# Attention b's output turned round by VectorE in blocks of 32 × 32 instead of by TensorE, in a kernel of four chained layers

## The chip, the cores and the metric

The kernel runs on one core of one Trainium2 chip. The metric is device time in microseconds (us), the median of several runs. Lower is better.

## The reference, cut to what matters

`x` has 4 batches × 256 tokens × 512 channels, in fp32. Four layers follow one another, each on the layernorm of `x` and added to `x`:

```
x = x + attn_a(layernorm(x))      # one head of 128
x = x + ffn(layernorm(x))         # int4 weights, dequantised
x = x + attn_b(layernorm(x))      # 32 heads of 16, rotary, causal
x = x + ffn(layernorm(x))         # the same weights again
# inside attn_b, for every batch:
q, k, v = x @ wq, x @ wk, x @ wv            # 512 -> 32 heads x 16
scores  = rotary(q) @ rotary(k).T / 4       # causal mask
out     = softmax(scores) @ v               # b, 256 tokens, 512
return out @ wo
# inside ffn: weight = (nibbles - zero) * scale, 512 x 512
```

## The kernel before, in words

Tokens lie on the 128 partitions, two tiles of 128 (t = 0, 1) to a batch. To multiply with a weight, the normalised activations `XN` are turned round by TensorE (step T), copied to `XT_hi` by ScalarE (TH, rounded to a short fp32 form) and the rest taken to `XT_lo` by VectorE (TL). Products then are two or three passes of TensorE over high and low parts (L816 to L818, L908 and L909).

Everything that is done is one step of a long hand-written list, `PLAN`, some 1,000 entries. Each engine walks through the list and issues its own steps in that order; waits between engines are semaphores, so an engine that waits holds up everything behind it in the list. `D` steps are loads, `OS` stores of the result, both on SyncE's queue. A function deals PSUM banks out in turn in the order of the list; in attention b's stretch three banks are kept for scores (S), three for the transposed scores (ST), and the other two serve all else.

Attention b works in 16 units u of 8 heads (four units for a batch), and each unit in two groups g of four heads:

- PJ projects queries and keys, RO, RP, P1, R1, P2, P3 apply the rotary table and split into three bf16 parts, SS and SL carry the parts through DRAM into `QK`. VP and VV make the values, 16 columns of values and 16 of ones for each head.
- S (L950, L952) makes scores and MX (L781) takes row maxima; MT, M1, M2, SM bring the maxima into `QK` as extra rows.
- ST (L973, L975) makes transposed scores less their maxima, EX (L667) exponentiates on ScalarE, MK (L547) masks on GpSimd, PV (L987) multiplies with the values. PV's result has 32 partitions for each of four heads (16 channels, and 16 rows that all hold the sum of the exponentials) and 256 tokens on the free axis.
- OU (ScalarE, two copies a unit, `OU`), NT (TensorE, L999, four transposes of 128 × 128 a unit) and NR (VectorE, L795 and L800: one reciprocal and two products) bring this to tokens on partitions and divide, into `O`.
- With all four units of a batch in `O`, DT (TensorE, L850, four transposes for each t), DH (ScalarE) and DL (VectorE, L720) turn it back to channels on partitions, high and low; WO (12 matmuls for each t, L816 to L818, 512 columns) multiplies with wo, OD (L757) adds to `X`.

Then layernorm LN (L714, L715), RS on GpSimd (four small steps with a power), NO on ScalarE (`XN`), T, TH, TL, the product F (L908, L909), and FS, FD (L744, L751, L753) on VectorE finish the batch, with BA (L515) on GpSimd. WT turns the int4 weights round once at the start (16 transposes, L835) after DQ unpacked them, and KP runs idle matmuls (L826) at the very start. The last steps of the list are those of batch 3.

## Time and profile before

| | |
|---|---|
| median of 3 runs | 287.44 us (287.19 to 287.57) |
| the profiled execution: own time, span | 289.1 us, 287.3 us |
| TensorE busy | 271.6 us (95% of the span) |
| VectorE busy | 211.5 us (74%) |
| GpSimd, ScalarE busy | 178.4 us, 155.6 us |
| granted TensorE clock, mean | 0.988 of full |

The span is what the rows of the trace cover; the execution's own time has 1.8 us around it. TensorE's busy time is the time in which at least one matmul was under way; matmuls overlap, so the mean duration of one is longer than the distance to the next.

### The profile page before, as it was taken

The page shows a single profiled execution, that of the slowest core. Times are in us where ns is not written, and L with a number is a line of the kernel's source. Part 1 is how long each engine was busy: PE and PEld are TensorE (multiplying, and loading weights), DVE is VectorE, ACT ScalarE, POOL GpSimd, SP SyncE. Part 2 cuts the span into 40 slices and gives each one's busy share as a digit, 9 for nine tenths or more (in the row PEclk, how much of TensorE's full clock was granted, in tenths as well). Part 3 has the DMA queues.
Part 4 walks back from the last instruction along what each step waited for, and adds up shares of the span by engine and source line. Part 5 has one row for each costly group of instructions (what it writes and reads, how often), then busy time and mean ns, then how long its engine had stood idle before and what let it go on. Part 6 is the DMA issues. An engine that isn't in the chain of part 4 may idle for free.

```text
span 287.3 us, 6794 instructions
## 1 busy us (share of the span) xinstructions
PE 271.6 (95%) x2444; PEld 225.9 (79%) x2444; DVE 211.5 (74%) x374; ACT 155.6 (54%) x263; POOL 178.4 (62%) x229
## 2 busy tenths in 40 slices
PE   7799999999999999999999999999999999986964
PEld 2688988898889988778798898887878878764852
DVE  2756498688899988968786868788759777444475
ACT  2668996545293445675415686273577435582040
POOL 5495779788974996775748981876465622470070
PEclk9999999999999999999999999999999999998699
DMA  6999150005654443324434344323453320012011
GB/s 167 341 381 346 46 113 1 2 25 150 181 138 97 130 112 97 100 80 121 128 97 130 103 133 123 103 62 94 111 158 93 103 68 3 1 40 110 3 73 73
DMA packets 50905, 31.88 MB, mean 111 GB/s; under 512 B 5368, under 2 KB 46008, under 8 KB 50872
## 3 DMA queue, kind: packets, MB, share of 16 engines
q1 hardware_dynamic: 50872, 31.44, 37.5%
q8 instruction: 20, 0.33, 0.5%
q14 instruction: 13, 0.11, 0.1%
HBM read 22.91 MB, written 8.39 MB: 109 GB/s over the span
## 4 chain that ended last, share of the span: by engine, by line
PE 89%; DVE 5%; issue 2%; ACT 2%; POOL 1%; DVEq 0%; POOLq 0%; ACTq 0%
PE psum L816 14%; PE psum L817 13%; PE psum L818 13%; PE psum L987 7%; PE psum L850 6%; PE psum L952 5%; PE psum L973 5%; PE psum L908 4%; PE psum L909 4%; PE psum L999 3%; PE psum L950 3%; PE psum L826 2%; PE psum L898 2%; PE psum L975 2%; PE psum L870 1%
## 5 line engine op out<-in xcount | busy, mean ns | idle before, releaser
L547 POOL TENSOR_SCALAR_AFFINE_SELECT E<-E 128x512 f32<-128x512 f32 x64 | 40.8, 662 | 45.8 <-ACT E L667 45.5
L781 DVE TENSOR_REDUCE nmax<-psum 128x4 f32<-128x512 f32 (+1 forms) x64 | 59.5, 946 | 4.5 <-PE psum L952 4.5
L667 ACT ACTIVATE E<-psum 128x1536 f32<-128x1536 f32 x32 | 46.3, 1447 | 15.2 <-PE psum L975 14.9
L816 PE MATMUL psum<-XT_lo,wb_hi 128*128 128x256 f32 x128 | 38.6, 301 | 0.0
L720 DVE TENSOR_TENSOR XT_lo<-psum,XT_hi 128x512 fp32r<-128x512 f32 x40 | 26.9, 683 | 14.1 <-ACT XT_hi L554 14.1
L817 PE MATMUL psum<-XT_hi,wb_lo 128*128 128x256 f32 x128 | 36.2, 282 | 0.0
L818 PE MATMUL psum<-XT_hi,wb_hi 128*128 128x256 f32 x128 | 36.1, 282 | 0.0
L576 ACT ACTIVATE XN<-X,offset,rstd 128x512 f32<-128x512 f32 x32 | 25.6, 809 | 16.7 <-POOL offset L509 16.6
L816 PE MATMUL psum<-wb_lo,XT_hi 128*128 128x256 f32 (+1 forms) x96 | 33.2, 346 | 0.3 <-DVE X L753 0.3
L554 ACT ACTIVATE XT_hi<-psum 128x512 fp32r<-128x512 f32 x40 | 23.3, 597 | 17.8 <-PE psum L850 17.6
L554 ACT ACTIVATE parts<-SH 128x512 bf16<-128x512 f32 x32 | 20.0, 626 | 21.0 <-POOL SH L536 15.4
L817 PE MATMUL psum<-wb_hi,XT_lo 128*128 128x256 f32 (+1 forms) x96 | 31.3, 326 | 0.0
L818 PE MATMUL psum<-wb_hi,XT_hi 128*128 128x256 f32 (+1 forms) x96 | 31.1, 323 | 0.0
L952 PE MATMUL psum<-QK 128*128 128x128 bf16 x256 | 29.8, 220 | 0.0
L987 PE MATMUL psum<-E,V 128*32 128x128 f32 (+1 forms) x512 | 26.9, 331 | 0.9 <-ACT V L554 0.8
L554 ACT ACTIVATE OU<-psum 128x256 f32<-128x256 f32 x32 | 12.1, 382 | 28.0 <-PE psum L987 27.8
L714 DVE BATCH_NORM_STATS2 stats<-X 128x6 f32<-128x512 f32 x32 | 21.9, 685 | 6.9 <-DMA X<-L_attn_a_x 6.4
L535 POOL TENSOR_TENSOR SH<-SH,table 128x512 f32<-128x512 f32 x16 | 20.9, 1306 | 9.6 <-DVE CC L768 9.5
L908 PE MATMUL psum<-wf,XT_lo 128*128 128x512 f32 x64 | 26.5, 414 | 0.4 <-DVE XT_lo L720 0.2
L816 PEld LDWEIGHTS psum<-XT_lo,wb_hi 128*128 128x128 f32 x128 | 24.4, 190 | 1.3 <-DVE XT_lo L720 0.7
L909 PE MATMUL psum<-wf,XT_hi 128*128 128x512 f32 x64 | 25.3, 395 | 0.0
L973 PE MATMUL psum<-QK 98*128 98x256 bf16 x128 | 24.7, 274 | 0.2 <-ACT E L667 0.2
(102 smaller groups left out, 697.5 us busy)
## 6 DMA issues: line engine op xcount, KB each, us to landing
QK<-qk_parts SPq DMA_DIRECT2D x192, 64.0 KB
qk_parts<-parts SPq DMA_DIRECT2D x16, 384.0 KB, 2.9
X<-L_attn_a_x SPq DMA_DIRECT2D x8, 256.0 KB, 5.9
out<-X SPq DMA_DIRECT2D x8, 256.0 KB, 2.2
wb_raw<-L_attn_b_wk SPq DMA_DIRECT2D x1, 1024.0 KB, 10.8
wb_raw<-L_attn_b_wv SPq DMA_DIRECT2D x1, 1024.0 KB, 13.1
wb_raw<-L_attn_b_wq SPq DMA_DIRECT2D x1, 1024.0 KB, 14.6
wb_raw<-L_attn_b_wo SPq DMA_DIRECT2D x1, 1024.0 KB, 14.6
```

What stands on the lines that cost most here:

```text
L547: last = nc.gpsimd.affine_select(out=e, in_=e, compare_op=ALU.is_ge, fill=0.0, base=0, pattern=[[0, GH], [1, P]], channel_multiplier=-1)
L554: return nc.scalar.activation(out_, in_, ACT.Copy)
L667: nc.scalar.activation(E[:, n % 2], bank(3, 3), ACT.Exp, scale=float(HD) ** -0.5).then_inc(done[k], 1)
L781: nc.vector.tensor_reduce(nmax[:, u % 2, g * GH:(g + 1) * GH, t], (bank(1, 2) if t else bank(0)).rearrange("p (h k) -> p h k", h=GH), AX, ...
L816: nc.tensor.matmul(out_, stat[0], mov[1], start=first, stop=False)
L817: nc.tensor.matmul(out_, stat[1], mov[0], start=False, stop=False)
L818: return nc.tensor.matmul(out_, stat[0], mov[0], start=False, stop=last)
L908: nc.tensor.matmul(ps, XT_lo[:, slot, kt, tok], wf[:, kt], start=kt == 0, stop=False)
L909: last = nc.tensor.matmul(ps, XT_hi[:, slot, kt, tok], wf[:, kt], start=False, stop=kt == KT - 1)
L952: last = nc.tensor.matmul(ps[:, (j + 1) * width - P:(j + 1) * width], q[:, h, t * P:width], kk[:, h, t * P:width], start=True, stop=True)
L973: nc.tensor.matmul(bank(3, 2)[:, j * S:(j + 1) * S], kk[0:SROWS, h, 0:P], q[0:SROWS, h, :], start=True, stop=True)
L987: last = nc.tensor.matmul(ps[j * 32:(j + 1) * 32, kt * P:S], values(u // 2)[:, kt, (u % 2) * UH + g * GH + j], E[:, n % 2, at:at + S - kt ...
```

## The change

What is divided is no longer turned round on TensorE. VectorE's transpose works on every square of 32 × 32 by itself. A unit's two groups now write to one bank (`PAIRS`), the heads are dealt to groups alternately (`h = NG * j + g`), and three steps on VectorE replace OU, NT and NR: NA transposes the 32 × 32 squares of the bank (128 × 512, PSUM to `TR`), after which a token's sum lies beside its channels, and takes the reciprocals (128 × 16); NX multiplies (128 × 256, `TR` to `TN`); NB transposes the squares back (128 × 256) into `O`, which now has channels on partitions. DT is gone: DH and DL read `O` in SBUF. The unpacked weights are bf16, and so are their transposes (WT). KP has 14 idle matmuls instead of 20 at the start, and stands three times more in batch 3's last pauses (4, 5 and 7 of them). After the last S the three score banks join the turn of the others. RS is split in two for one more batch. PLAN is a new list.

```diff
         E = sb("E", [P, 2, GH * 3 * P], F32)
-        OU = sb("OU", [P, NG, S], F32)
+        TR = sb("TR", [P, NG * S], F32)
+        TN = sb("TN", [P, S], F32)
+        inv_o = sb("inv_o", [P, NG, S // 32], F32)
         parts = sb("parts", [P, 2, 3, 2 * S], BF16)
...
-                elif k == "OU":
-                    u, g = st[1:]
-                    act.wait_ge(done["PV"], upto("PV", u, g))
-                    if u:
-                        act.wait_ge(done["NT"], upto("NT", u - 1))
-                    copy(OU[:, g], bank(bank_of["PV", u, g])[:, 0:S]).then_inc(done[k], 1)
...
+                elif k == "DH":
+                    b, t = st[1:]
+                    act.wait_ge(done["NB"], last_of(*[("NB", KT * b + m) for m in range(KT)]))
...
+                    copy(xt_half(XT_hi, st), O[:, :, t * P:(t + 1) * P]).then_inc(done[k], 1)
...
+                elif k == "DL":
+                    hi, t = ("DH", *st[1:]), st[2]
+                    dve.wait_ge(done["DH"], upto(*hi))
+                    nc.vector.tensor_tensor(xt_half(XT_lo, hi), O[:, :, t * P:(t + 1) * P],
+                                            xt_half(XT_hi, hi).bitcast(F32), ALU.subtract).then_inc(done[k], 1)
...
+                elif k == "NA":
+                    u = st[1]
+                    dve.wait_ge(done["PV"], last_of(*[("PV", u, g) for g in range(NG)]))
+                    if u:
+                        dve.wait_ge(done["NX"], upto("NX", u - 1))
+                    link(nc.vector.transpose(TR[:], bank(bank_of["PV", u, 0])))
+                    nc.vector.reciprocal(inv_o[:], TR[:].rearrange("p (g i d) -> p g i d", g=NG, d=2 * HD)[:, :, :, HD]
+                                         ).then_inc(done[k], 1)
+                elif k == "NX":
+                    u = st[1]
+                    dve.wait_ge(done["NA"], upto("NA", u))
+                    if u:
+                        dve.wait_ge(done["NB"], upto("NB", u - 1))
+                    tr = TR[:].rearrange("p (g i d) -> p i g d", g=NG, d=2 * HD)
+                    nc.vector.tensor_tensor(TN[:].rearrange("p (i g d) -> p i g d", g=NG, d=HD), tr[:, :, :, 0:HD],
+                                            inv_o[:].rearrange("p g i -> p i g").unsqueeze(3).to_broadcast(
+                                                (P, S // 32, NG, HD)), ALU.mult).then_inc(done[k], 1)
+                elif k == "NB":
                     u = st[1]
                     b, m = divmod(u, KT)
-                    dve.wait_ge(done["NT"], upto("NT", u))
-                    ps = bank(bank_of["NT", u]).rearrange("p (g t h d) -> p g t h d", g=NG, t=NT, h=GH)
-                    inv = inv_o[:].rearrange("p (g t h) -> p g t h", g=NG, t=NT)
-                    link(nc.vector.reciprocal(inv, ps[:, :, :, :, HD]))
+                    dve.wait_ge(done["NX"], upto("NX", u))
                     if m == 0 and b:
-                        dve.wait_ge(done["DT"], last_of(*[("DT", b - 1, t) for t in range(NT)]))
-                    for t in range(NT):
-                        o = O[:, t, m * P:(m + 1) * P].rearrange("p (g h d) -> p g h d", g=NG, h=GH)
-                        last = nc.vector.tensor_tensor(
-                            o, ps[:, :, t, :, 0:HD],
-                            inv[:, :, t, :].unsqueeze(3).to_broadcast((P, NG, GH, HD)), ALU.mult)
-                    last.then_inc(done[k], 1)
+                        dve.wait_ge(done["DL"], last_of(*[("DL", b - 1, t) for t in range(NT)]))
+                    nc.vector.transpose(O[:, m], TN[:]).then_inc(done[k], 1)
 
...
                 if k == "KP":
...
-                    for _ in range((20, 24)[st[1]]):
...
+                    for _ in range(st[1]):
...
                 elif k == "WT":
...
-                    ps = take(st)
+                    ps = take(st).bitcast(BF16)
...
-                                                   ident[:])
+                                                   ident_h[:])
...
                 elif k == "PV":
...
-                    ps = take(st)
+                    ps = (bank(bank_of["PV", u, 0]) if g else take(st))[:, g * S:(g + 1) * S]
...
-                elif k == "NT":
-                    u = st[1]
-                    pe.wait_ge(done["OU"], last_of(*[("OU", u, g) for g in range(NG)]))
-                    ps = take(st)
-                    for g in range(NG):
-                        for t in range(NT):
-                            c = (g * NT + t) * P
-                            last = nc.tensor.transpose(ps[:, c:c + P], OU[:, g, t * P:(t + 1) * P], ident[:])
```

How the list of before and of the change stand on VectorE in attention b's stretch: before, unit 0's NR (L795, L800) among row maxima (MX, L781) and other batches' layernorm.

```order
L787 TENSOR_TENSOR mrow<-psum,mrow 16x128
L795 RECIPROCAL inv_o<-psum 128x16
L800 TENSOR_TENSOR O<-psum,inv_o 128x128 x2
L781 TENSOR_REDUCE nmax<-psum 128x4 x2
L714 BN_STATS stats<-X 128x6
L715 BN_AGGR mv<-stats 128x2
L774 TENSOR_TENSOR parts<-SH,parts 128x512
L720 TENSOR_TENSOR XT_lo<-psum,XT_hi 128x4x128
L767 STREAM_SHUFFLE SH<-psum 128x512
```

In the changed kernel the same engine has, for units 1 to 3, NA (L807, L808), NX (L816) and NB (L825), with MX now at L794:

```order
L794 TENSOR_REDUCE nmax<-psum 128x4
L816 TENSOR_TENSOR TN<-TR,inv_o 128x256
L807 STREAM_TRANSPOSE TR<-psum 128x512
L808 RECIPROCAL inv_o<-TR 128x16
L825 STREAM_TRANSPOSE O<-TN 128x256
L728 TENSOR_TENSOR XT_lo<-psum,XT_hi 128x4x128
L794 TENSOR_REDUCE nmax<-psum 128x4
L728 TENSOR_TENSOR XT_lo<-psum,XT_hi 128x4x128
L816 TENSOR_TENSOR TN<-TR,inv_o 128x256
L807 STREAM_TRANSPOSE TR<-psum 128x512
L808 RECIPROCAL inv_o<-TR 128x16
L825 STREAM_TRANSPOSE O<-TN 128x256
```

Where a unit had three instructions of NR it has four, of more elements, and units 1 to 3 follow one another closely.

VectorE at the end of the list: before, from unit 15's NR on.

```order
L795 RECIPROCAL inv_o<-psum 128x16
L800 TENSOR_TENSOR O<-psum,inv_o 128x128 x2
L720 TENSOR_TENSOR XT_lo<-psum,XT_hi 128x4x128 x3
L757 TENSOR_TENSOR X<-X,psum 128x512
L714 BN_STATS stats<-X 128x6
L715 BN_AGGR mv<-stats 128x2
L757 TENSOR_TENSOR X<-X,psum 128x512
L714 BN_STATS stats<-X 128x6
```

In the changed kernel, from unit 15's NA on, where L728 is TL and L733 DL:

```order
L728 TENSOR_TENSOR XT_lo<-psum,XT_hi 128x4x128
L807 STREAM_TRANSPOSE TR<-psum 128x512
L808 RECIPROCAL inv_o<-TR 128x16
L816 TENSOR_TENSOR TN<-TR,inv_o 128x256
L825 STREAM_TRANSPOSE O<-TN 128x256
L733 TENSOR_TENSOR XT_lo<-O,XT_hi 128x4x128
L757 SCALAR_TENSOR_TENSOR X<-shift_r,row_sum,X 128x512
L733 TENSOR_TENSOR XT_lo<-O,XT_hi 128x4x128
L770 TENSOR_TENSOR X<-X,psum 128x512
L723 BN_STATS stats<-X 128x6
L724 BN_AGGR mv<-stats 128x2
L770 TENSOR_TENSOR X<-X,psum 128x512
```

Batch 2's T (t = 1) and its TL now stand ahead of unit 15's division, and t = 0 comes first in DL and OD.

TensorE at the end: before, from unit 15's last PV on to the first matmuls of WO.

```order
L987 MATMUL psum<-E,V 32x256 x4
L987 MATMUL psum<-E,V 32x128 x4
L999 MATMUL psum<-ident,OU 128x128 x4
L850 MATMUL psum<-ident,O 128x128 x8
L850 MATMUL psum<-ident,XN 128x128 x4
L816 MATMUL psum<-wb_lo,XT_hi 128x512
L817 MATMUL psum<-wb_hi,XT_lo 128x512
```

In the changed kernel from unit 15's last PV on: the product F of batch 2 (four pairs of L922 and L923), four idle matmuls (L848), then WO (L838 to L840).

```order
L1001 MATMUL psum<-E,V 32x256 x4
L1001 MATMUL psum<-E,V 32x128 x4
L922 MATMUL psum<-wf,XT_lo 128x512
L923 MATMUL psum<-wf,XT_hi 128x512
L922 MATMUL psum<-wf,XT_lo 128x512
L923 MATMUL psum<-wf,XT_hi 128x512
L922 MATMUL psum<-wf,XT_lo 128x512
L923 MATMUL psum<-wf,XT_hi 128x512
L922 MATMUL psum<-wf,XT_lo 128x512
L923 MATMUL psum<-wf,XT_hi 128x512
L848 MATMUL psum<-ident_h 128x512 x4
L838 MATMUL psum<-wb_lo,XT_hi 128x512
```

NT, DT and T are gone from this place, and F has taken it; WO (24 matmuls) is followed by five idle matmuls, T, seven idle matmuls and T.

TensorE at the start: before, the first rows up to the first product of attention a.

```order
L826 MATMUL psum<-ident_h 128x512 x20
L850 MATMUL psum<-ident,XN 128x128 x8
L816 MATMUL psum<-XT_lo,wqkv_hi 128x256
L817 MATMUL psum<-XT_hi,wqkv_lo 128x256
```

In the changed kernel the weights' transposes (L855) stand ahead of it, in bf16:

```order
L848 MATMUL psum<-ident_h 128x512 x14
L864 MATMUL psum<-ident,XN 128x128 x12
L855 MATMUL psum<-ident_h,w_f 128x128 x12
L864 MATMUL psum<-ident,XN 128x128 x4
L855 MATMUL psum<-ident_h,w_f 128x128 x4
L838 MATMUL psum<-XT_lo,wqkv_hi 128x256
L839 MATMUL psum<-XT_hi,wqkv_lo 128x256
```

On VectorE the unpacking of the weights (DQ) stands now ahead of the second TL of batch 0 and of QL, which the first product of attention a waits for.

## Rows read from the trace of the kernel before

**Rows 1.** The page's first line of busy time by engine.

```profile
PE 271.6 (95%) x2444; PEld 225.9 (79%) x2444; DVE 211.5 (74%) x374; ACT 155.6 (54%) x263; POOL 178.4 (62%) x229
```

**Rows 2.** Busy time in four stretches (us, instructions), PEclk, DMA share, GB/s.

```profile
75.00:244.00 169.00, 167.53 (x1721) 140.78 (x1719) 137.16 (x240) 91.72 (x140) 108.22 (x129) 1.00 0.39 106
80.00:100.00 20.00, 19.97 (x197) 18.28 (x197) 19.66 (x32) 11.54 (x20) 13.26 (x16) 1.00 0.49 118
260.80:287.30 26.50, 17.65 (x72) 13.52 (x72) 14.89 (x24) 5.18 (x10) 5.17 (x10) 0.87 0.19 70
265.00:270.00 5.00, 4.35 (x13) 3.54 (x13) 1.91 (x3) 1.19 (x2) 0.00 (x0) 0.50 0.01 2
```

**Rows 3.** Groups by line: count, busy us, mean ns of one, idle before.

```profile
L720 DVE TENSOR_TENSOR XT_lo<-psum,XT_hi 128x512 fp32r<-128x512 f32 x40 | 26.9, 683 | 14.1 <-ACT XT_hi L554 14.1
...
L774 DVE TENSOR_TENSOR parts<-SH,parts 128x512 bf16<-128x512 f32 x16 | 14.4, 902 | 0.6 <-ACT parts L554 0.6
...
L767 DVE STREAM_SHUFFLE SH<-psum 128x512 f32<-128x512 f32 x16 | 11.9, 742 | 0.1
...
L999 PE MATMUL psum<-ident,OU 128*128 128x128 f32 x64 | 9.9, 277 | 1.1 <-DVE X L753 0.9
...
L800 DVE TENSOR_TENSOR O<-psum,inv_o 128x128 f32<-128x128 f32 x32 | 7.8, 285 | 0.6
...
L850 PE MATMUL psum<-ident,O 128*128 128x128 f32 x32 | 5.5, 310 | 0.9 <-DVE O L800 0.9
...
L795 DVE RECIPROCAL inv_o<-psum 128x16 f32<-128x16 f32 x16 | 4.1, 255 | 10.4 <-PE psum L999 10.4
...
L693 DVE CAST w_f<-w_int 128x2048 f32<-128x2048 int32 x1 | 1.2, 1226 | 0.0
L696 DVE TENSOR_TENSOR wqkv_lo<-wqkv_raw,wqkv_hi 128x1024 fp32r<-128x1024 f32 x1 | 1.2, 1224 | 0.1
...
L692 DVE TENSOR_SCALAR w_int<-q_int 128x1024 int32<-128x1024 int32 x1 | 0.7, 690 | 0.0
```

**Rows 4.** TensorE's timeline at unit 0's NT: start, length, instruction.

```profile
105.12 0.63 PE L999 MATMUL psum<-ident,OU 128*128 128x128 f32 x4
105.58 0.22 PE L950 MATMUL psum<-QK 96*128 96x128 bf16 x1
105.64 0.22 PE L952 MATMUL psum<-QK 128*128 128x128 bf16 x1
```

**Rows 5.** VectorE's timeline at unit 0's NR, same columns.

```profile
105.78 0.26 DVE L795 RECIPROCAL inv_o<-psum 128x16 f32<-128x16 f32 x1
106.08 0.49 DVE L800 TENSOR_TENSOR O<-psum,inv_o 128x128 f32<-128x128 f32 x2
106.48 1.81 DVE L781 TENSOR_REDUCE nmax<-psum 128x4 f32<-128x1024 f32 x2
```

**Rows 6.** TensorE's timeline at the start, same columns.

```profile
1.98 7.09 PE L826 MATMUL psum<-ident_h 128*128 128x512 bf16 x20 [1.98 <-POOL ident_h L493]
8.90 1.04 PE L850 MATMUL psum<-ident,XN 128*128 128x128 f32 x8
11.51 0.39 PE L816 MATMUL psum<-XT_lo,wqkv_hi 128*128 128x256 f32 x1 [1.57 <-DVE XT_lo L720]
```

**Rows 7.** The chain that ended last, its last 26 us: start, us, engine, line.

```profile
261.63 0.64 PE psum L999 x4
...
266.76 0.53 PE psum L816
267.29 0.43 PE psum L817
...
273.69 0.24 PE psum L818
273.96 0.70 DVE X L757
...
284.18 0.69 DVE X L753
```

More of the change, by code:

```diff
@@ L88 @@
 PLAN = [
[130 rows of a table removed]
[126 rows of a table added]
 ]
 READ_BY = {"WT": "WC", "T": "TL", "QK": "QC", "QV": "VC", "SA": "AE", "VA": "AC", "ET": "EC", "OA": "OC", "WA": "WD",
[L223 removed]
+           "F": "FD", "PJ": "RO", "VP": "VV", "MT": "M2", "PV": "NA", "WO": "OD"}
+PAIRS = ("PJ", "VP", "PV")
 def bank_turns():
[L228 to L229 removed]
+    bank_of, before, owner, pool, turn = {}, {}, [None] * BANKS, range(BANKS), 1
+    last_s = max(i for i, st in enumerate(PLAN) if st[0] == "S")
+    for i, st in enumerate(PLAN):
         k = st[0]
[L231 removed]
+        if k == "S" and k not in before:
             before[k], pool = [o for o in owner[:3] if o], range(3, BANKS)
[L233 removed]
+        if k == "ST" and k not in before:
             before[k], pool = [o for o in owner[3:6] if o], range(6, BANKS)
[L235 removed]
+        if i == last_s:
+            pool, owner[:3] = [*pool, 0, 1, 2], [("MX", *st[1:3], t) for t in (0, 1, 1)]
+        if k == "KP":
+            bank_of[st], before[st] = 5, owner[5] if len(pool) == BANKS else ("EX", NU - 1, NG - 1)
+            continue
+        if k not in READ_BY or (k in PAIRS and st[2]):
             continue
@@ L247, in xt_turns @@
     for st in PLAN:
-        if st[0] not in ("T", "DT"):
+        if st[0] not in ("T", "DH"):
             continue
@@ L342, in hybrid_block_kernel @@
         mrow = sb("mrow", [UH * NT, 2, 2, P], BF16)
-        inv_o = sb("inv_o", [P, NG * NT * GH], F32)
         scratch = nc.dram_tensor("qk_parts", (2, 3, 2, P, S), BF16, kind="Internal").ap()
-        done = {k: sem(f"done_{k}") for k in count if k not in ("D", "QM", "SS", "SL", "SM", "OS")}
+        done = {k: sem(f"done_{k}") for k in count if k not in ("D", "KP", "QM", "SS", "SL", "SM", "OS")}
         loaded = {st[1:]: sem("loaded_" + "_".join(map(str, st[1:]))) for st in PLAN if st[0] == "D"}
@@ L567, in _ @@
                     act.wait_ge(done["WT"], upto("WT", st[1]))
-                    copy(wf[:, st[1]], bank(bank_of["WT", st[1]])).then_inc(done[k], 1)
+                    copy(wf[:, st[1]], bank(bank_of["WT", st[1]]).bitcast(BF16)[:, 0:C]).then_inc(done[k], 1)
                 elif k == "NO":
@@ L824, in _ @@
                     ps = take(st)
-                    for _ in range((20, 24)[st[1]]):
-                        last = nc.tensor.matmul(ps.rearrange("p (j n) -> p j n", n=P), ident_h[:],
-                                                ident_h[:].unsqueeze(1).to_broadcast((P, BANK // P, P)),
-                                                start=True, stop=True)
-                    last.then_inc(done[k], 1)
+                    for _ in range(st[1]):
+                        nc.tensor.matmul(ps.rearrange("p (j n) -> p j n", n=P), ident_h[:],
+                                         ident_h[:].unsqueeze(1).to_broadcast((P, BANK // P, P)), start=True, stop=True)
                 elif k == "WT":
```

57 lines of the change are left out of this document (22 added, 35 removed), and 256 rows, old and new, of the table PLAN.

## The prediction

> **What bounds the kernel now.** I read the busy line first: TensorE is busy 95% of the span, VectorE 74% [rows 1]. A mean over stages says little, so the busy time by stretch came next. From 75 to 244 us TensorE is busy 167.5 of 169 us and VectorE 137.2 of them [rows 2]: in this long middle each us taken off TensorE is a us of the end, if the other engines follow. VectorE has 31.8 us free there, and the stretch from 80 to 100 us shows both nearly full at once, 19.97 and 19.66 of 20 us, so a full VectorE does not by itself hold TensorE up [rows 2]. The last 26.5 us are another regime: TensorE is busy 17.7 us at a mean clock of 0.87, VectorE 14.9, neither full [rows 2]. There the chain of waits rules. It goes through unit 15's NT, the turning back, WO, and batch 3's layernorm and product [rows 7]. The start is a third regime: idle matmuls from 1.98 us for 7.09 us, two T, then a wait until 11.51 us for VectorE [rows 6]. So I cost the change in three parts. The profiled execution took 289.1 us, of which the span is 287.3; the median of the runs is 287.44. I take the change of the span off the median.
>
> **Part 1: TensorE's work until unit 15's last PV.** Four transposes of NT start at 105.12 and the next step's first matmul at 105.58 [rows 4]: 0.46 us a step, though the records are busy 0.63. Ahead of the end phase stand 15 of the 16 NT: 15 × 0.46 = 6.9 us removed. DT has 24 of its 32 transposes there, as six steps of the same form: 6 × 0.46 = 2.8 us removed. WT's 16 transposes keep their number but become bf16. As fp32 they cost 4 × 0.46 = 1.8 us; bf16 matmuls of 128 columns follow one another at 0.06 us (105.58 to 105.64) [rows 4], so 16 × 0.06 = 1.0 us, 0.8 saved. If bf16 does nothing for a transpose, 0.8 is lost again. One T of batch 2 (0.46) moves from the end phase to ahead of it. Sum: 6.9 + 2.8 + 0.8 − 0.46 = 10.0 us less. The copies OU on ScalarE, also gone, are not on the path: nothing is taken for them.
>
> **Part 2: the start.** Fourteen idle matmuls at the mean distance of 0.355 us (7.09 / 20) end at 7.0 us; at 0.43 us, if all ran at the lower clock, at 8.0 [rows 6]. The weights' unpacking (two operations of 0.69 us, a cast of 1.23) now stands on VectorE ahead of the second TL and of QL (1.22) [rows 3], and its input is loaded ahead of wqkv. No row shows when that input would be in; I choose 9 us, the time of the first T now. Then the chain is 9 + 2.6 + 0.7 (TL) + 1.2 = 13.5 us for attention a's first product, against 11.51 before [rows 3, 6]. But by then TensorE has done four T and four WT, 4 × 0.46 + 1.0 = 2.8 us of its work, against two T (0.9 us) before. Idle time at the start is 13.5 − 2.8 = 10.7 against 11.51 − 0.9 = 10.6: no gain by this sum. The first T no longer stands behind the idle matmuls until 8.90, so what follows it has more room: I take 0.3 us gained. Bounds: 1.5 us gained if the weights arrive early, 2 us lost if they are late.
>
> **Part 3: VectorE in the middle.** A unit's NR takes 0.70 us (105.78 to 106.48) [rows 5]. NA, NX and NB are not in this trace. The nearest to a transpose of 128 × 512 out of PSUM is the shuffle of 128 × 512 out of PSUM, 0.74 us [rows 3]. From 285 ns for 128 elements and 683 for 512 [rows 3] an element costs 1.04 ns, so 256 elements cost 0.42. The reciprocal of 16 elements took 0.26 [rows 3]. That is 0.74 + 0.26 + 0.42 + 0.42 = 1.84, less 0.09 for overlap (the two L800 take 0.49 us in place of 2 × 0.285 [rows 3, 5]): 1.75 us, so 1.05 more a unit. Fourteen units in the middle add 14.7 us to 137.2, in a stretch that TensorE leaves after some 169 − 10 = 159 us: 151.9 of 159, 96% busy. Lower bound of the price: a transposed element at half the cost, 0.35 less a unit. Upper: twice the cost of the transposes (0.74 + 0.42 = 1.16 more a unit), or GpSimd in the way: the subtraction of P3, whose operands all lie in SBUF, takes 902 ns on the mean where the same size with an operand in PSUM takes 683 [rows 3], and NX, NB and DL have all operands in SBUF too; at 902 / 683 that is 0.3 us more a unit. I take the middle price.
>
> What does 96% cost? I laid both lists out in portions of 15 us of TensorE's work, with VectorE's steps in them at the durations above. Before, the fullest portion has 16.7 us of VectorE to 15.9 of TensorE. In the change three portions are over: 17.1 to 15.6, 16.8 to 16.2, 18.1 to 15.2. The excess is 1.5 + 0.6 + 2.9 = 5.0 us. Part of it is absorbed by what VectorE has ready ahead (the portion ahead of the last has 10.1 to 12.9), as it is now from 80 to 100 us. I take 2.0 us lost; bounds 0 and 5.0, or 8 and more at the doubled price. Queued behind an NA that waits are MX and TL, and TensorE waits for both: S for MX's banks, the products for TL.
>
> By the Trainium skill (VectorE: DVE Perf Modes, The three transpose paths) VectorE's transpose of 128 × 128 bf16 takes 311 ns; stretched to 512 elements at its own clock that is an estimate of 0.71 us, near the shuffle's row. The same page (Rules for kernel authors) says to transpose 128 × 128 on TensorE where PSUM is fine as a destination, and to keep the count of chained VectorE operations low, which speaks against this change: a unit goes from three instructions to four. By the rows the trade is 0.46 us and more of TensorE's time a unit for 1.05 of VectorE's, and TensorE's is the dear one.
>
> **Part 4: the end.** Before, from 260.8 to 266.76, when WO begins, there are 6.0 us: OU, NT, NR, DT, DH, DL of both tiles, and a T [rows 7]. The change has NA 0.74 + 0.26, NX 0.42, NB 0.42, DH 0.60, DL 0.68 and six hand-overs at 0.06: 3.5 us [rows 3]. Hidden beside it on TensorE are the product F (eight matmuls, 1.9 us) and four idle matmuls, about 1 us. Then WO: before, its 24 matmuls take 266.76 to 273.93, since the first stand 0.43 apart, at a clock of 0.50 from 265 to 270, which is the lower of the two levels (1.2 GHz); the last take 0.24 [rows 2, 7]. TensorE had been mostly waiting for 5 us ahead of that. In the change it works through 2.9 of those 3.5 us, so I take 24 × 0.24 = 5.7 us. WO's end falls at 9.2 us into the phase, against 13.1. What follows, from OD (273.96) to the last FD's end (284.18 + 0.69 = 284.87), is 10.9 us, then 2.4 for the store [rows 2, 7]. The order there is nearly the same, but tile 0 leads, and FD of batch 2 does not stand between: I take 10.4. End phase: 9.2 + 10.4 + 2.4 = 22.0 against 26.5: 4.5 us less. The idle matmuls ahead of T cost nothing as long as NO is later than they are (NO comes about 3 us behind OD). Bounds: 2.5 less, if the clock falls all the same (1.8 us of WO), 5.5 if FS and BA are out of the way.
>
> **Sum.** −10.0 − 0.3 + 2.0 − 4.5 = −12.8 us: a span of 274.5, and a median of 287.44 − 12.8 = 274.6 us.
>
> **The rivals.** (a) VectorE becomes the bound. For it: 96% as worked out, and a price never seen in this trace. With transposes at twice the shuffle's rate, 1.05 + 1.16 = 2.2 more a unit, 14 units add 31 us: 168 us of VectorE in a stretch of 159. Then 9 us and the usual waits are lost in place of 2.0, and the median is 282 to 284; with GpSimd in the way alone, 14 × 0.3 = 4.2 us more of VectorE's time, three quarters of which I would expect to see: 278. Against it: the shuffle, which also moves between partitions, costs only 0.06 us more than a plain copy's size. (b) The new start is late: thin work between 8 and 13 us lets the clock fall to 1.2 GHz as it did at 265 us, and attention a's first products stand twice as far apart for some 4 us. It costs 1.8 us, as WO did: 276.4 us. For it: four pauses in a row; against: the pause up to 11.51 did not lower the clock [rows 6]. (c) Slower than before: the transposes of 4-byte elements run several times slower than the shuffle. VectorE's free 31.8 us and the end's gain of 4.5 make this decide at (31.8 + 4.5) / 14 = 2.6 us more a unit, transposes at 2.3 times the row. At four times (3.5 more, 4.5 in all) 14 units add 63 us: 200 us in place of 169, less 4.5: 314 us. Nothing in the rows speaks for it. (d) No crowding at all and the start early: 287.44 − 10.0 − 1.5 − 4.5 = 271.4 us.
>
> **How the numbers follow.** The forecast (within 271.4 and 277.5, with d and b in it) has 0.65, (a) 0.29, (c) 0.04, and a change that comes to nothing, in pauses that I don't see, 0.02. The predicted time is that of the forecast's sum. The range from 270 to 281 leaves out the upper part of (a), and (c). Under 0.2% (0.6 us) a change of this kernel can't be told from none: faster 0.95, same 0.01, slower 0.04.
>
> **What would show it.** Transposes near 0.74 and 0.42 us; VectorE 225 to 230 us busy; TensorE's busy time 10 to 13 us lower and still over 97% in the middle; WO's first matmul 3.5 us after the last PV, 0.24 apart; the first product of attention a near 13.5 us. The prediction is wrong if TensorE shows waits for row maxima (S for MX) or TL of more than 4 us in the middle, if the transposes are dearer, or if the clock is low at the end.

## The result, and the profile after

The changed kernel takes 280.25 us in the median of 4 runs (279.60 to 280.61), the kernel before 287.50 in the 4 runs beside it (287.19 to 289.20): ratio 0.9724, interval 0.9688 to 0.9759, 7.25 us less. The forecast was 274.6 with a range of 270 to 281. The sign was right and the time is inside the range, but 5.65 us, four tenths of the forecast gain, are missing. The profiled execution took 280.3 us with a span of 278.3. In two of the kernels below one run lay more than 1.5% above the fastest of its kernel (286.56 and 292.14 us), and it is left out of their medians.

The busy line of the page, beside [rows 1]: TensorE is busy 12.4 us less and VectorE 16.4 us more.

```profile
PE 259.2 (93%) x2358; PEld 212.6 (76%) x2358; DVE 227.9 (82%) x390; ACT 145.0 (52%) x231; POOL 180.8 (65%) x233
```

The windows of the change (length, then busy us of PE, PEld, DVE, ACT and POOL, PEclk, DMA share, GB/s): from attention a's first product to unit 15's last PV, most of the middle, and the end phase.

```profile
14.67:256.09 241.42, 234.34 (x2240) 197.09 (x2240) 205.43 (x353) 133.00 (x212) 168.23 (x195) 1.00 0.37 111
75.00:236.00 161.00, 155.50 (x1633) 130.39 (x1632) 147.82 (x248) 83.52 (x118) 105.75 (x125) 1.00 0.40 114
256.09:278.30 22.21, 16.55 (x73) 10.99 (x72) 13.87 (x24) 4.16 (x8) 4.74 (x10) 1.00 0.13 47
```

The first of these stretches in the kernel before, from its own first product at 11.51 us to its last PV:

```profile
11.51:260.80 249.29, 246.00 (x2344) 208.92 (x2344) 191.90 (x340) 144.99 (x247) 167.25 (x195) 1.00 0.38 110
```

The last PV ends 4.7 us earlier (256.09 against 260.80). TensorE is idle 241.42 − 234.34 = 7.1 us in the stretch, before it was 3.3. The end phase is 22.2 us against 26.5 [rows 2]. What TensorE waited for, from the list of its waits (total, times, longest):

```profile
PE psum L864 <- ACT XN L585: 3.0, 2, 1.5
PE psum L987 <- DMA QK<-mrow: 2.4, 3, 1.3
...
PE psum L838 <- issue: 1.5, 1, 1.5
PE psum L966 <- DMA QK<-qk_parts: 1.4, 2, 0.9
...
PE psum L964 <- DVE nmax L794: 0.4, 1, 0.4
```

The first and the third are at the start. The other two are new: S waits for the stacks of queries and keys (SL), ST for the rows of maxima (SM). Both are transfers, both issued by SyncE, and nothing in the prediction had them. The waits that it feared, S for MX (0.4 us) and TL (about 1 us in all), hardly show.

The new operations, by line:

```profile
L807 DVE STREAM_TRANSPOSE TR<-psum 128x512 f32<-128x512 f32 x16 | 11.4, 711 | 1.1 <-PE psum L1001 0.4
...
L816 DVE TENSOR_TENSOR TN<-TR,inv_o 128x256 f32<-128x256 f32 x16 | 10.3, 641 | 0.3
...
L825 DVE STREAM_TRANSPOSE O<-TN 128x256 f32<-128x256 f32 x16 | 6.9, 430 | 0.2
```

TensorE's timeline at the start: four T and four WT, with three pauses between them, stand where two T and one pause stood [rows 6].

```profile
1.98 5.16 PE L848 MATMUL psum<-ident_h 128*128 128x512 bf16 x14 [1.98 <-POOL ident_h L502]
...
9.05 0.63 PE L864 MATMUL psum<-ident,XN 128*128 128x128 f32 x4 [1.48 <-ACT XN L585]
11.18 0.63 PE L864 MATMUL psum<-ident,XN 128*128 128x128 f32 x4 [1.50 <-ACT XN L585]
11.64 0.83 PE L855 MATMUL psum<-ident_h,w_f 128*128 128x128 bf16 x12
...
14.67 0.36 PE L838 MATMUL psum<-XT_lo,wqkv_hi 128*128 128x256 f32 x1 [1.46 <-issue]
```

And the chain of the end, beside [rows 7]: unit 15's NA, NX, NB, DH, DL, then WO at the full clock from its second matmul on.

```profile
255.76 0.68 DVE XT_lo L728
256.44 0.63 DVE TR L807
257.10 0.26 DVE inv_o L808
257.39 0.43 DVE TN L816
257.85 0.46 DVE O L825
258.33 0.64 ACT XT_hi L563
258.99 0.70 DVE XT_lo L733
259.74 0.50 PE psum L838
260.24 0.23 PE psum L839
```

### The profile page after: what moved, and what is told of

Its sections match the earlier page's. It is cut to its first block, busy times and chain, and to the rows that moved or that the text cites. A ratio compares the mean times of both kernels' runs of the same rounds, so it can differ in the third digit from the quotient of the medians.

```text
span 278.3 us, 6590 instructions
## 1 busy us (share of the span) xinstructions
PE 259.2 (93%) x2358; PEld 212.6 (76%) x2358; DVE 227.9 (82%) x390; ACT 145.0 (52%) x231; POOL 180.8 (65%) x233
## 4 chain that ended last, share of the span: by engine, by line
PE 73%; SPq 8%; DMA 7%; DVE 6%; issue 3%; ACT 1%; POOL 1%; DVEq 0%; POOLq 0%
PE psum L838 12%; PE psum L839 11%; PE psum L840 11%; SPq L467 6%; PE psum L1001 5%; PE psum L922 5%; PE psum L923 5%; PE psum L864 4%; PE psum L987 4%; PE psum L966 4%; PE psum L912 3%; DMA QK<-mrow 2%; PE psum L964 2%; PE psum L989 2%; DMA QK<-qk_parts 2%
## 5 line engine op out<-in xcount | busy, mean ns | idle before, releaser
L556 POOL TENSOR_SCALAR_AFFINE_SELECT E<-E 128x512 f32<-128x512 f32 x64 | 40.1, 652 | 37.1 <-ACT E L682 37.0
L794 DVE TENSOR_REDUCE nmax<-psum 128x4 f32<-128x512 f32 (+1 forms) x64 | 59.5, 943 | 2.5 <-PE psum L966 2.3
L838 PE MATMUL psum<-XT_lo,wb_hi 128*128 128x256 f32 x128 | 38.6, 301 | 0.0
L840 PE MATMUL psum<-XT_hi,wb_hi 128*128 128x256 f32 x128 | 36.1, 282 | 0.0
L838 PE MATMUL psum<-wb_lo,XT_hi 128*128 128x256 f32 (+1 forms) x96 | 31.9, 333 | 0.5 <-DVE inv_o L808 0.3
L840 PE MATMUL psum<-wb_hi,XT_hi 128*128 128x256 f32 (+1 forms) x96 | 30.6, 318 | 0.0
L839 PE MATMUL psum<-wb_hi,XT_lo 128*128 128x256 f32 (+1 forms) x96 | 30.6, 318 | 0.0
L728 DVE TENSOR_TENSOR XT_lo<-psum,XT_hi 128x512 fp32r<-128x512 f32 x32 | 21.5, 683 | 10.5 <-ACT XT_hi L563 10.2
L544 POOL TENSOR_TENSOR SH<-SH,table 128x512 f32<-128x512 f32 x16 | 21.9, 1366 | 10.9 <-DVE CC L781 10.8
L922 PE MATMUL psum<-wf,XT_lo 128*128 128x512 f32 x64 | 26.3, 410 | 0.7 <-DVE XT_lo L728 0.5
L838 PEld LDWEIGHTS psum<-XT_lo,wb_hi 128*128 128x128 f32 x128 | 24.4, 190 | 1.4 <-issue 0.6
L923 PE MATMUL psum<-wf,XT_hi 128*128 128x512 f32 x64 | 25.3, 395 | 0.0
L839 PEld LDWEIGHTS psum<-XT_hi,wb_lo 128*128 128x128 f32 x128 | 24.4, 191 | 0.5 <-issue 0.4
L563 ACT ACTIVATE XT_hi<-psum 128x512 fp32r<-128x512 f32 x32 | 18.5, 596 | 12.1 <-PE psum L864 12.0
## 6 DMA issues: line engine op xcount, KB each, us to landing
wb_raw<-L_attn_b_wq SPq DMA_DIRECT2D x1, 1024.0 KB, 11.4
wb_raw<-L_attn_b_wv SPq DMA_DIRECT2D x1, 1024.0 KB, 12.4
```

What stands on the lines that cost most here:

```text
L556: last = nc.gpsimd.affine_select(out=e, in_=e, compare_op=ALU.is_ge, fill=0.0, base=0, pattern=[[0, GH], [1, P]], channel_multiplier=-1)
L563: return nc.scalar.activation(out_, in_, ACT.Copy)
L794: nc.vector.tensor_reduce(nmax[:, u % 2, g::NG, t], (bank(1, 2) if t else bank(0)).rearrange("p (h k) -> p h k", h=GH), AX, ALU.max, negat ...
L838: nc.tensor.matmul(out_, stat[0], mov[1], start=first, stop=False)
L839: nc.tensor.matmul(out_, stat[1], mov[0], start=False, stop=False)
L840: return nc.tensor.matmul(out_, stat[0], mov[0], start=False, stop=last)
```

## The experiments

Each run has the kernel before timed beside it on the same chip (medians of 287.4 to 288.5 us there); differences below a microsecond between kernels are read with the ratios' intervals. For each kernel whose middle matters I give the window from its first product of attention a to its last PV; its length and TensorE's idle time in it are the two numbers to compare with 241.42 and 7.1 us of the change. These come from one execution each. The kernel before gave 249.29 us in both of its profiled executions. The change without its idle matmuls at the end, whose steps on TensorE are the same up to the last PV, gave 240.83 us with 6.6 us idle in place of 241.42 and 7.1:

```profile
14.60:255.43 240.83, 234.20 (x2240) 197.04 (x2240) 205.35 (x353) 133.00 (x212) 168.24 (x195) 1.00 0.38 112
```

So a difference of 0.6 us between two such windows can be chance.

**The kernel before, once more.** No edit.

> The kernel before, unchanged, to see whether its first profiled execution (289.1 us, clock 0.50 from 265 to 270 us) stands for its median (287.4 us). Theory: it does not; the low clock at WO's first matmuls comes in some executions only, so the spans of the other executions are some 1.6 us shorter with a clock near 1.00, and the end phase before is 25 us and not 26.5. Rival: every execution has the low clock at the end, spans are near 287 us and clocks 0.988 in all of them.

288.28 us (10 runs) against 288.53: ratio 1.0002, interval 0.9974 to 1.0029. Its profiled execution took 287.44 us, 1.7 less than the one that the prediction read. The idle matmuls of the start lasted 6.16 us instead of 7.09, so the first product came at 10.65 instead of 11.51 and all behind it 0.86 earlier; and at the end seven matmuls of WO, not nine, ran 0.43 apart (the clock here is the lower level, 1.2 GHz):

```profile
266.00:268.00 2.00, 2.00 (x6) 1.59 (x5) 0.54 (x1) 0.00 (x0) 0.00 (x0) 0.50 0.00 0
```

The granted clock's rise at the start and its fall at the end move from execution to execution. The expectation was half right: this execution is 1.7 us shorter, but the low clock at WO is there too, and the end phase takes 25.7 us (259.89 to 285.6), not 25. The prediction took a change of span worked out against a long execution off a median of three shorter ones: that is 1.7 us of the 5.65. The three were themselves short. The medians of the kernel before beside the later runs are 288.53, 288.33, 287.91 and 287.44 us, so the execution of 289.1 us was only some 0.6 to 0.8 us above the two of these with the most runs (13 and 19).

**The new method in the old order.** The changed kernel with the list of before: NA where the second OU stood, NX and NB in NR's place, NT and DT gone, 20 idle matmuls at the start and none at the end. The two banks that serve all else are no longer dealt in turn: a step gets the one whose last reader stands first in the list. Two other pieces differ from the old list: three units have the order of their PVs exchanged, and four steps of TensorE stand a little later, behind the readers of their banks.

```diff
-    ("OU", u, 1), ... ("NT", u), ("NR", u), ...
+    ("NA", u), ... ("NX", u), ("NB", u), ...
```

> The new method (NA, NX, NB, bf16 weights' transposes, bank pairs) in the list of before, with no idle matmuls at the end. Theory that the method alone brings TensorE's 10 us: 10 us of TensorE's work less, VectorE crowded where the old list is full already (80 to 120 us), so 279 to 283 us. Rival, that the new order is what makes the method pay: 284 to 288 us, with TensorE waiting for row maxima and TL.

308.78 us, ratio 1.0680 (1.0631 to 1.0729): 20 us slower than before, where the theory had 279 to 283 us and its rival 284 to 288. In the window

```profile
10.80:278.59 267.79, 239.47 (x2261) 199.19 (x2262) 207.26 (x355) 134.29 (x216) 168.33 (x196) 1.00 0.34 102
```

TensorE is idle 28.3 us, and VectorE isn't full either: 207 of 268 us. The two wait for each other, TensorE in the window mostly for VectorE's RO, M2 and NA, and VectorE for TensorE (the residual's addition 13.0 us, NA 10.9):

```profile
DVE X L772 <- PE psum L842: 13.0, 6, 4.8
DVE TR L809 <- PE psum L1003: 10.9, 5, 4.6
```

So the method pays only with the new order: nearly the same instructions take 28 us more in the old list. NA waits in VectorE's queue for the last PV, and whatever stands behind it waits too. The opposite (old method, new order) wasn't run, so what the new order is worth by itself isn't known.

**No idle matmuls at the end.**

```diff
+PLAN = [st for st in PLAN if st[0] != "KP" or len(st) == 2]
```

> The changed kernel without its 16 idle matmuls at the end. If they hold the clock: the clock falls at WO or at the last T and F, 1.5 to 4 us slower (282 to 284 us). If the shorter pauses alone hold it: same time, 280.2 us, or up to 0.9 us faster, since the five and seven idle matmuls stood ahead of T in the chain that ended last.

280.55 us (3 runs, 280.06 to 282.23), ratio 0.9729 (0.9688 to 0.9770), against 280.25 and 0.9724 of the change. In the profiled execution, from WO's first matmul to the last FD's end it takes 17.06 us (259.08 to 276.14) against 16.15 (259.74 to 275.89). Its chain shows why: two pauses of 1.45 and 2.09 us, and then T and the last product's first matmuls at half speed.

```profile
264.82 1.45 issue
266.27 0.63 PE psum L866 x4
266.90 2.09 issue
268.98 1.08 PE psum L866 x4
270.07 0.43 PE psum L924
```

The sixteen matmuls are worth about 0.9 us in this execution; the medians differ by 0.3 us, which is inside the interval. WO itself ran 0.23 apart without the four ahead of it, so it is the product F, not the idle matmuls, with which its full clock goes together.

**Idle matmuls in the end of the kernel before.** Nine, three each ahead of unit 15's NT, of DT(3,0) and of T(4,2,1).

```diff
-                    for _ in range((20, 24)[st[1]]):
+                    for _ in range(3 if st[1] else 20):
```

> The kernel before with nine idle matmuls in the three pauses ahead of WO (three ahead of unit 15's NT, of DT and of batch 2's T). If they hold the clock, WO's first seven to nine matmuls stand 0.23 apart in place of 0.43 and it is 1.4 to 1.8 us faster than before (286.8 us against 288.5), which is the part of the change's gain that a held clock explains. If the clock falls all the same, or they delay the transposes, same or up to 0.7 us slower.

287.69 us against 288.33, ratio 0.9970 (0.9948 to 0.9991). WO now ran 0.23 apart, but the clock fell later: from 276 to 278 us it is 0.50, and the last product begins 0.43 apart. What the filling of one pause gave was mostly lost at the next. Of the change's 4.3 us at the end I put the clock between 0.6 us (this run) and 1.8 (nine matmuls 0.2 us slower each [rows 7]), as an estimate; the rest is the shorter chain.

**The first transpose twice, and one transpose less.** The first run does NA's transpose two times (same data). The second leaves NB's out, so that NX's product is written straight to `O` and the output isn't the reference's.

```diff
                     link(nc.vector.transpose(TR[:], bank(bank_of["PV", u, 0])))
+                    link(nc.vector.transpose(TR[:], bank(bank_of["PV", u, 0])))
```

> The changed kernel with the first transpose (128 x 512 out of PSUM) of each unit done twice: 0.74 us of VectorE more a unit, 11.9 us in all, nothing else changed. If VectorE is what bounds the middle, 8 to 12 us slower (288 to 292 us). If the middle's waits come from SyncE's queue and the landing of DMAs, VectorE still has slack and it costs 1 to 5 us.

> The changed kernel without NB: the product is written straight into O, the second transpose (0.43 us a unit, 6.9 us of VectorE in all) is left out, so what goes on into WO is not the reference's. Doubling the first transpose cost 5.9 us for 11.4 us of VectorE's time, a slope of one half. If VectorE's load holds the middle up in the changed kernel as it stands, 2 to 4 us faster (276.5 to 278.5 us, of which 0.4 in the end phase, where NB is in the chain). If the waits that are left come from SyncE's queue, only the end phase's 0.4 to 0.6 us.

The sixteen transposes more take 11.4 us, but VectorE's busy time grew by 8.9 (236.8 against 227.9); the time grew by 5.9 us (286.14, ratio 0.9906, 0.9873 to 0.9939). The sixteen less had taken 6.9 us, but NX, now writing to `O`, takes 714 ns on the mean in place of 641, and VectorE's busy time fell by 4.9 (to 223.0); the time fell by 1.2 (279.06, ratio 0.9675, 0.9643 to 0.9706), of which about 0.45 is the transpose in the end's own chain. The windows:

```profile
14.21:260.23 246.02, 235.81 (x2240) 196.98 (x2240) 213.64 (x368) 132.88 (x212) 167.97 (x195) 1.00 0.37 110
```

```profile
13.93:255.36 241.43, 234.54 (x2240) 197.15 (x2240) 201.21 (x338) 133.02 (x213) 168.38 (x195) 1.00 0.37 112
```

Upward VectorE decides (8.2 us more of it, the stretch 4.6 us longer), downward it doesn't (4.2 us less): 241.43 us is the change's own length, idle time 6.9. Something else holds there.

**VectorE's part nearly away.** NA transposes 128 × 256 straight into `O` (into `TN` in three units, and from there with a second one); reciprocal, product and the other transposes are left out, so the output isn't the reference's.

```diff
-                    link(nc.vector.transpose(TR[:], bank(bank_of["PV", u, 0])))
+                    nc.vector.transpose(TN[:] if b and m == 0 else O[:, m],
+                                        bank(bank_of["PV", u, 0])[:, 0:S]).then_inc(done[k], 1)
```

> The change, but VectorE's part for attention b is one transpose of half a bank a unit (128x256, 0.43 us); the reciprocal, the product and the second transpose are left out (two units more steps stay in three units, 0.43 us each), so the output isn't the reference's. VectorE loses about 25 us of its 228. Theory V (the middle's waits of 4.1 us more than before come from VectorE being crowded): nearly all of them go, and 1.3 us at the end where the reciprocal and the product of the last unit are in the chain: 280.2 - 4 - 1.3 = about 275. Rival Q (they come from SyncE's queue and from the transfers of the stacks that lie ahead of the small ones): the waits on QK stay, and 277.5 to 278.5 comes out. The run with one transpose less gave 1.2 us for 6.9 us of VectorE; at that slope 25 us would give 4.4 us, 275.8, in between, so the waits named in the trace decide.

279.37 us, ratio 0.9684 (0.9632 to 0.9736), 0.9 less than the change. The window and the waits:

```profile
14.51:255.78 241.27, 233.93 (x2240) 197.09 (x2240) 185.96 (x311) 132.67 (x212) 167.71 (x195) 1.00 0.38 111
```

```profile
PE psum L953 <- DMA QK<-qk_parts: 2.8, 3, 1.2
...
PE psum L974 <- DMA QK<-mrow: 1.5, 2, 0.9
```

VectorE lost 19.5 us in the stretch and the stretch didn't get shorter. The waits for the stacks grew from 1.4 to 2.8 us, those for the maxima's rows fell from 2.4 to 1.5. VectorE's crowding, to which the prediction gave its 2.0 us, isn't what holds the stretch up when it is lifted alone.

**Half of the stacks' transfers.** From unit 4 on six and not twelve transfers a unit; the rows left out keep an earlier unit's low-order parts, so the output isn't quite the reference's.

```diff
-                        for row, c in enumerate(which):
+                        for row, c in enumerate(which[:6 if u < QK_SLOTS else 3]):
```

> The change, but from the fifth unit on each unit's stacks are loaded by six transfers and not twelve (the first three groups of rows of queries and of keys; the other rows keep an earlier unit's parts, so the output isn't the reference's). SyncE loses 12 x 6 x 0.55 = 40 us of issuing and the queue half of its bytes. Rival Q (queue and transfers): the waits on QK<-mrow (2.4 us) and on QK<-qk_parts (1.4 us) go, 280.2 - 3.5 = about 276.7. Theory V (VectorE and the order set them): the row of the mask still comes late from VectorE, only its landing is shorter, and what is saved comes back as waits elsewhere: 279 to 280.2.

280.24 us, ratio 0.9723: nothing. The waits for the stacks are gone, that for the maxima's rows stays (2.3 us). Its profiled execution (281.56, where two others took 279.72 and 279.82) had the clock down from 12 to 19 us, so its window holds 2.3 us more of busy time (236.63 against 234.34). Without them it is 240.6 us long, 0.8 shorter than the change's, little more than two windows of one middle differ by chance.

```profile
14.48:257.42 242.94, 236.63 (x2240) 199.30 (x2240) 204.90 (x353) 132.46 (x212) 168.37 (x195) 0.99 0.31 92
```

**Both at once**, on the start of the last run below (278.53 us), so that the clock doesn't blur it. What is left out is what the two runs leave out.

> The two runs before it in one (one transpose of half a bank a unit on VectorE, half of the transfers of the stacks from the fifth unit on; the output isn't the reference's), on the start with its idle matmuls in the pauses (278.5 us), so that no fall of the clock blurs it. Each alone gave 0.4 to 0.9 us, and in each the waits on the other side stayed or grew (small VectorE: QK loads 4.3 us against 3.8; half the loads: 2.3 us on the row of the mask). Theory J (VectorE's work and SyncE's transfers are two supplies of about equal lateness, and with one lifted the other one holds): together they give back most of the middle's 4 us and 1.1 us at the end, 278.5 - 3 - 1.1 = about 274.4. Rival O (neither; the order of the list and the row's own chain through ScalarE and VectorE set the waits): the end's 1.1 us and little more, 277 to 277.4.

274.71 us (274.55 to 274.87), ratio 0.9545 (0.9501 to 0.9590), 3.8 us under that base.

```profile
13.98:251.37 237.39, 233.52 (x2240) 197.19 (x2240) 184.96 (x311) 132.24 (x212) 167.53 (x195) 1.00 0.32 94
```

The stretch is 4.0 us shorter than the change's, and 2.9 shorter than that of its base (240.33); of the 2.9, 1.8 us are idle time of TensorE and the rest is busy time. TensorE is idle 3.9 us in it, nearly the 3.3 of before. In the medians the two gave 0.9 and 0.0 us alone and give 3.8 together. The reading that fits is that two supplies are about equally late: VectorE's steps, which end with M2 and P3, and SyncE's transfers, which take their results on. One rival is left. The pair ran on another start than the two single runs, and that start by itself had already brought the idle time from 7.1 to 5.6 us; neither was run alone on it. That the two together give back most of the new idle time is shown, that each alone would do nothing there is not.

**The rows' transfers from ScalarE.** SM's two transfers move from SyncE to ScalarE, each behind ScalarE's next step after M2.

```diff
-                elif k == "SM":                      # in SyncE's program
+                elif k == "SM":                      # in ScalarE's program, nc.scalar.dma_start
```

> The changed kernel with the two small DMAs of SM (the maxima's rows) issued from ScalarE's queue, each behind ScalarE's next step after M2, instead of from SyncE behind the twelve DMAs of SL. Theory that SyncE's queue makes ST late: the waits for QK from mrow (2.4 us) and part of those for qk_parts (1.4) go, 1 to 3.5 us faster (277 to 279 us). Rival: ScalarE now waits for M2 itself and issues for 1.1 us a unit, EX comes later, and it is 0 to 5 us slower.

289.31 us (9 runs, 287.68 to 291.86), ratio 1.0039 (0.9999 to 1.0079): the whole gain is gone, more than the 0 to 5 us of its rival.

```profile
14.57:266.49 251.92, 237.87 (x2240) 199.56 (x2240) 204.31 (x353) 133.46 (x213) 167.59 (x195) 0.99 0.36 106
```

TensorE waits 6.8 us for the maxima's rows in place of 2.4, and once 2.7 us for a row maximum. The transfers landed no sooner (2.4 us in the median against 2.0, 3.2 to 4.5 us in the chain), and in ScalarE's order they stand behind its activations: the chain goes through one of E (102.46 us) to an issue whose transfer lands 3.22 us after 103.35. The queue was no free place, and the test says little on SyncE itself; the pair of runs above does that.

**The start.** First QH (the split of attention a's weights) ahead of the normalization NO(1,1,1) on ScalarE, nothing else:

```diff
-    ("D", "q"), ("DQ",), ..., ("NO", 1, 1, 1), ("D", "wqkv", 1), ("TL", 1, 0, 0), ("QH",), ...
+    ("D", "q"), ("DQ",), ..., ("QH",), ("NO", 1, 1, 1), ("D", "wqkv", 1), ("TL", 1, 0, 0), ...
```

> The changed kernel with one step of the list moved: QH (wqkv's rounding on ScalarE) ahead of batch 1's NO instead of behind it. The start's chain is QH, QL, first product of attention a; its input lands near 9.8 us while QH starts at 12.12. If this chain sets when TensorE becomes full, the first product moves from 14.67 to about 13.9 us and all behind it 0.7 us earlier (279.5 us). If the middle's waits decide on their own, no difference.

280.21 us, ratio 0.9711: nothing. The first product came at 14.21 us, 0.46 earlier. That is less than expected, and no more than the scatter: in the six other kernels with the change's own start it came at 13.93 to 14.60. QL, which the first product waits for, began at 11.80 in place of 13.20, but took 2.31 us in place of 1.37, beside GpSimd's addition of the bias (BA, 11.75 to 13.03). And the clock had fallen. The windows show 0.92 and 0.50 (the lower level, 1.2 GHz):

```profile
10.00:12.00 2.00, 1.20 (x12) 1.02 (x13) 1.97 (x4) 2.00 (x4) 0.25 (x1) 0.92 0.74 173
12.00:14.00 2.00, 2.00 (x15) 1.59 (x12) 2.00 (x1) 2.00 (x5) 1.03 (x1) 0.50 1.06 400
```

The window up to the last PV is no shorter either, with 7.9 us idle:

```profile
14.21:256.98 242.77, 234.89 (x2240) 197.71 (x2240) 205.63 (x353) 132.56 (x212) 168.15 (x195) 1.00 0.38 111
```

Then the same with idle matmuls in the pauses:

```diff
     ("T", 1, 0, 1),
+    ("KP", 5, 8),
...
     ("T", 1, 0, 0),
+    ("KP", 4, 9),
...
     ("T", 1, 1, 0),
+    ("KP", 2, 10),
```

> The change with the split of q's weights ahead of the last normalization of the start, as in the run before of that kind, and 5, 4 and 2 idle matmuls more behind the first three transposes of the inputs, where TensorE waited 1.5, 0.9 and 0.3 us and the granted clock fell to 0.50 from 12 to 15 us. If the fall of the clock ate what the earlier start gave (first product at 14.21 against 14.67 us, but four products at the low clock behind it), the first product comes at 13.7 us at the full clock and the time is 0.8 us under the change: 279.4. If a start that is earlier only makes the transfers of the rows late against TensorE (waits on QK<-mrow rose from 2.4 to 2.8 us and on QK<-qk_parts from 1.4 to 1.7), nothing is left of it: 280.2.

278.53 us (278.09 to 279.70, 6 runs), ratio 0.9666 (0.9635 to 0.9697), 1.7 less than the change, and the fastest kernel of this study that computes the reference. TensorE's timeline:

```profile
9.57 0.63 PE L864 MATMUL psum<-ident,XN 128*128 128x128 f32 x4 [0.40 <-ACT XN L585]
10.04 1.03 PE L848 MATMUL psum<-ident_h 128*128 128x512 bf16 x4
...
13.75 0.36 PE L838 MATMUL psum<-XT_lo,wqkv_hi 128*128 128x256 f32 x1 [0.19 <-issue]
```

The first product is at 13.75 us, the mean clock of the execution 1.00. In this one QL takes 1.22 us and GpSimd's BA beside it 2.35, the other way round. From the first product to the last PV it takes 240.33 us, another 1.1 less than the change, with 5.6 us idle; the waits on transfers are 1.7 us in place of 3.8. That an earlier start shifts them favourably here, and didn't in the run before, is seen but not explained.

## Why the prediction was right or wrong

The forecast had the mechanism right, and its time came inside the range because the range was wide: 5.65 us of 12.8 are missing. Of the signs that it named, the durations, VectorE's 227.9 us, TensorE's 12.4 us less and WO at 3.65 us hold; TensorE is busy 96.6% of the middle (155.50 of 161 us), not over 97%, and the first product came 1.2 us late. The profiled spans, 287.3 to 278.3, divide into work −9.8, start +1.3, idle time behind it +3.8 and end −4.3, sum −9.0. Against the forecast's −12.8:

- **Part 1, TensorE's work, −10.0: right.** The end of the last PV moved by −4.7 us; with the start's +1.3 and the idle time's 7.1 − 3.3 = +3.8 this leaves −9.8 for the work. The bf16 transposes of the weights follow one another at 0.06 us (twelve from 11.64 to 12.36), as forecast.
- **Part 2, the start, −0.3: wrong by 1.6 us.** The step that failed is the chain "9 + 2.6 + 0.7 (TL) + 1.2 = 13.5 us". The first product came at 14.67 with 2.8 us of work done ahead of it, 11.9 us idle against 10.6. TL was done at 12.24, as the chain had it, but QL started only at 13.20, because the split's first half (QH, 12.12 to 13.16) stood on ScalarE behind a normalization that the sum hadn't counted. Some 0.6 us of this varies between executions: a step of RS on GpSimd (L517) took 1.25 us in this one and 0.70 in six of the others, and in one of the six, the kernel with one transpose less, QL started at 12.61 and the first product came at 13.93. With the split ahead and the pauses filled the forecast's 13.5 is nearly met (13.75). Another 0.3 us had been taken as a gain without a row. Rival (b), the low clock, didn't happen in the change's profiled execution, but it did in those of two variants (the weights' split first, half of the transfers), in just such thin work. The second suggests the price: 281.56 us beside 279.72 and 279.82, near the rival's 1.8.
- **Part 3, VectorE in the middle, +2.0: the size half of it, the cause half.** Durations were right: 0.71, 0.25, 0.42 in the median (0.64 in the mean) and 0.43 us. VectorE was less full in the middle than forecast, 147.8 of 161 us or 92% in place of 96%, and the idle time grew more all the same. The step that failed is "The excess is 1.5 + 0.6 + 2.9 = 5.0 us", as a thing of VectorE alone. I read only compute engines. SyncE's queue, whose transfers before had cost TensorE almost nothing, became late at the same moment. Measured +3.8 us, and neither VectorE's work (0.15 us of the stretch for 19.5 of VectorE) nor the transfers (0.8) gives it back alone on the change's start, while both give 2.9 us of the stretch on the start with its pauses filled, which gave 1.1 by itself. Rival (a) in its milder form, 278 us by GpSimd in the way, came near the time by another way: beside GpSimd, NX costs 0.22 us a unit more on the mean than in the median, 3.5 us of VectorE's time, of which two instructions have 3.0; P3, whose 902 ns the price came from, took 775, which gave 2.0 us back.
- **Part 4, the end, −4.5: right** (−4.3). WO starts 3.65 us after the last PV (forecast 3.5), its matmuls stand 0.23 apart. NA waited 0.3 us for a TL ahead of it.
- **The median.** "I take the change of the span off the median" cost 1.7 us, since the profiled execution of before was 1.7 us over its median (0.86 of it at the start, the rest in the end phase) and that of the change was at its median (280.3 and 280.25). Start 1.6, idle time 1.8, work 0.2, end 0.2 and this 1.7 add up to 5.5 of the 5.65 us. Since the three executions of the median were short ones, some 0.9 of the 1.7 (288.3 − 287.44) is the bad luck of that sample.

Left open: why the old order loses so much more (28 us idle) than the count of VectorE's work would give, as no run separates the banks from the queue; what the new order is worth without the new method; and what either supply is worth alone on the filled start.

## What to carry to other kernels

When work moves off the bound engine, the next bound can be two suppliers at once. Lifting either alone then shows next to nothing, so run both together, and each alone on the same base. Cost the issuing queue like an engine: the twelve transfers of a unit occupy SyncE for 5.5 to 7 us, before and after, and a small transfer that TensorE needs can stand behind them. Compare an execution with the median of more than three runs before you subtract. Where new steps leave pauses at the start, try filling them: here that and one step moved gave 1.7 us. A method and its order are one change: the same steps in the old list lost 20 us.

## What the runs showed of the hardware

A product of 256 elements, all operands in SBUF, takes 0.41 us, but at 130.31 it took 2.49. VectorE's timeline, and below it GpSimd's:

```profile
130.31 2.49 DVE L816 TENSOR_TENSOR TN<-TR,inv_o 128x256 f32<-128x256 f32 x1
132.91 0.72 DVE L807 STREAM_TRANSPOSE TR<-psum 128x512 f32<-128x512 f32 x1
...
133.84 0.39 DVE L825 STREAM_TRANSPOSE O<-TN 128x256 f32<-128x256 f32 x1
134.32 1.34 DVE L816 TENSOR_TENSOR TN<-TR,inv_o 128x256 f32<-128x256 f32 x1
```

```profile
130.15 2.37 POOL L533 TENSOR_TENSOR wb_lo<-wb_raw,wb_hi 128x1024 fp32r<-128x1024 f32 x1
132.99 2.40 POOL L533 TENSOR_TENSOR wb_lo<-wb_raw,wb_hi 128x1024 fp32r<-128x1024 f32 x1 [0.46 <-ACT wb_hi L563]
```

GpSimd's subtraction runs from 130.15 to 132.52, and VectorE's product, begun at 130.31, ends 0.28 us behind it; the second product, begun within the next subtraction (to 135.39), ends 0.27 us behind that. Two transposes, one from PSUM and one from SBUF to SBUF, run at their usual length (0.72 and 0.39 us) beside the second subtraction. The Trainium skill (SBUF — State Buffer, SBUF: two separate sides) says that the port pair which VectorE and GpSimd share is an exclusive lock, held for a whole instruction, and that a VectorE operation with two SBUF inputs takes part in it against a GpSimd operation that reads SBUF. The trace agrees for the two products, which ended 0.28 and 0.27 us behind GpSimd; the transpose within SBUF, with one input, was not held up.

The time that a transfer's issue takes is a second thing that I hadn't looked for. The chain around the wait at 114.56 us, SyncE's part of it (start, length); the first is one of the twelve issues of a unit's stacks (most take 0.43 us), the second that of the maxima's row:

```profile
109.29 0.90 SPq L467
...
110.77 0.51 SPq L475
...
111.32 3.20 DMA QK<-mrow
```

M2 had finished at 108.95; the row was issued at 110.77, behind the stacks, and landed 3.2 us after the issue where the median landing is 2.0. The Trainium skill (DMA: Bandwidth & Descriptors, Issuing engines are not separate DMA queues) says that transfers issued from several engines run on the same 16 DMA engines, so that another issuer saves issue time alone; the run with the rows on ScalarE agrees, its landings are no shorter (2.4 us in the median against 2.0).
